# Attention over 1024 positions on one core: two PSUM banks in turn for the projection groups, and the running sum of the probabilities in SBUF

## What is computed

```
B, C, H, W = 16, 512, 32, 32;  N_HEADS = 8;  d_k = 64
xr = x.reshape(B, C, S).transpose(0, 2, 1)                      # S = 1024
q, k, v = split((xr @ w_qkv + b_qkv).reshape(B, S, 8, 192), 3)
attn = softmax(einsum('bihd,bjhd->bijh', q, k) * d_k ** -0.5, over j)
out = einsum('bijh,bjhd->bihd', attn, v).reshape(B, S, 512) @ w_proj + b_proj
return out.transpose(0, 2, 1).reshape(B, C, H, W) + x
```

## Time and profile before

| | |
|---|---|
| median of 2 runs | 3987.8 us (3986.29 to 3989.31) |
| profiled execution | 3987.98 us |
| its span | 3985.9 us |
| granted TensorE clock, mean | 0.997 |

### The profile page before, as it was taken

One profiled execution on the slowest core, in us unless ns is written; L12 is line 12 of the kernel. 1 busy time (PEld: TensorE's weight loads), 2 busy tenths in 40 slices (PEclk: granted clock), 3 DMA queues, 4 the chain that ended last, 5 costly groups with the idle time before them and its releaser, 6 DMA issues.

```text
span 3985.9 us, 60063 instructions
## 1 busy us (share of the span) xinstructions
PE 3936.3 (99%) x18464; PEld 3360.4 (84%) x18464; DVE 3319.5 (83%) x4449; ACT 2935.8 (74%) x5529; POOL 3006.5 (75%) x2371
## 2 busy tenths in 40 slices
PE   8999999999999999999999999999999999999998
PEld 6878888888888888888888888888888888888886
DVE  7788888888888888888888888888888888888887
ACT  5777777777777777777777777777777777777775
POOL 4678777777777777777777777877778777787775
PEclk9999999999999999999999999999999999999999
DMA  6344444434443344443444444444344434444432
GB/s 201 85 108 112 125 107 110 118 95 132 110 120 104 99 131 112 111 113 96 132 105 127 107 107 111 116 128 107 95 121 112 129 100 108 112 110 127 113 93 79
DMA packets 262943, 451.23 MB, mean 113 GB/s; under 512 B 107872, under 2 KB 118112, under 8 KB 258656
## 3 DMA queue, kind: packets, MB, share of 16 engines
q1 hardware_dynamic: 262624, 447.39, 42.4%
HBM read 204.48 MB, written 41.42 MB: 62 GB/s over the span
## 4 chain that ended last, share of the span: by engine, by line
PE 89%; issue 4%; DVE 4%; ACT 2%; DMA 1%; POOL 0%; SPq 0%; ACTq 0%; DVEq 0%
PE ps_g L473 24%; PE s L495 11%; PE ps_o L517 11%; PE ps_o L515 11%; PE st L574 11%; PE st L572 10%; PE ps_g L489 9%; DVE acc L806 2%; PE st L501 1%; PE st L502 1%; ACT p_hl L731 1%; ACT x_h L690 1%; ACT p L728 0%; DVE acc L803 0%; DVE qk_l L787 0%
## 5 line engine op out<-in xcount | busy, mean ns | idle before, releaser
L963 POOL TENSOR_TENSOR p_hl<-p,p_hl 128x512 fp32r<-128x512 f32 x2048 | 2609.0, 1298 | 915.0 <-ACT p_hl L731 914.4
L728 ACT ACTIVATE p<-st 128x512 f32<-128x512 f32 x2048 | 1231.8, 601 | 705.3 <-PE st L574 678.5
L809 DVE TENSOR_REDUCE nm<-s 128x1 fp32r<-128x1024 f32 x1024 | 1250.1, 1221 | 381.6 <-PE s L495 370.8
L806 DVE TENSOR_TENSOR acc<-acc,p 128x512 f32<-128x512 f32 x1792 | 1234.1, 689 | 25.5 <-DVE acc L803 0.5
L731 ACT ACTIVATE p_hl<-st 128x512 fp32r<-128x512 f32 x2048 | 1237.7, 604 | 0.0
L515 PE MATMUL ps_o<-p_hl,v_hl 128*128 128x512 f32 x2048 | 802.9, 392 | 4.5 <-POOL p_hl L963 3.9
L574 PE MATMUL st<-q,k 128*128 128x512 f32 x2048 | 804.4, 393 | 0.0
L517 PE MATMUL ps_o<-p_hl,v_hl 128*128 128x512 f32 x2048 | 802.0, 392 | 0.0
L572 PE MATMUL st<-q,k 128*128 128x512 f32 x2048 | 799.6, 390 | 1.4 <-DVE v_hl L794 1.1
L473 PE MATMUL ps_g<-x_h,wq 128*128 128x512 f32 x2016 | 711.5, 393 | 6.4 <-DVE qk_l L787 6.3
L495 PE MATMUL s<-k,q 128*128 128x512 f32 x2048 | 646.7, 396 | 9.0 <-DMA k<-qk_l 4.7
(11 more groups left out here) (192 smaller groups left out, 3756.8 us busy)
## 6 DMA issues: line engine op xcount, KB each, us to landing
k<-qk_h SPq DMA_DIRECT2D x256, 256.0 KB, 4.3
wq<-wq_d SPq DMA_DIRECT2D x126, 512.0 KB, 4.5
ring<-x_in SPq DMA_DIRECT2D x128, 256.0 KB, 3.7
q<-qk_h SPq DMA_DIRECT2D x128, 256.0 KB, 3.8
q<-qk_l SPq DMA_DIRECT2D x128, 256.0 KB, 4.9
k<-qk_l SPq DMA_DIRECT2D x128, 256.0 KB, 5.1
q<-q SPq DMA_DIRECT2D x256, 128.0 KB, 4.9
rinv<-rinv_d SPq DMA_DIRECT2D x256, 128.0 KB, 2.9
```

The costliest lines, as they stand in the source:

```text
L728: nc.scalar.activation(p[:, to, :], st[slot % RING][:], ACT.Exp)
L806: nc.vector.tensor_tensor(acc[:], acc[:], probs, ALU.add).then_inc(acc_done, 1)
L809: nc.vector.tensor_reduce(nm[:, it:it + 1], s1[:], AXX, ALU.max, negate=True).then_inc(max_done, 1)
L963: nc.gpsimd.tensor_tensor(p_l[:, to, :], p[:, to, :], p_h[:, to, :].bitcast(f32), ALU.subtract).then_inc(pl_done, 1)
```

## The change

`acc` becomes a tile in SBUF, and its bank becomes a second one for groups: `ps_g` is now a list of two. The method `bank` gives the bank of a unit: how many groups begin up to it, modulo 2. `held` becomes a dictionary that keeps, for each bank, the semaphore and the value that its last reader will have set; TensorE waits for it when a group begins in that bank, which is the group before the last one.

```
+        def bank(self, unit):
+
+            return sum(begin <= unit for begin in GROUP) % 2
...
+        acc = sb("acc", [P, HALF])
...
-        acc = ctx.enter_context(nc.psum_tensor("acc", [P, HALF], f32))
-        ps_g = ctx.enter_context(nc.psum_tensor("ps_g", [P, HALF], f32))
-        qk_banks = [ps_o, acc, st[0], st[1]]
-        v_banks = [ps_g, st[2], ps_o, acc]
-        out_banks = [ps_g[:], st[1][:], st[2][:], s1[:, cols(0)], s1[:, cols(1)], ps_o[:], acc[:], st[0][:]]
+        ps_g = [ctx.enter_context(nc.psum_tensor(f"ps_g{i}", [P, HALF], f32)) for i in range(2)]
+        qk_banks = [ps_o, ps_g[1], st[0], st[1]]
+        v_banks = [ps_g[0], st[2], ps_o, ps_g[1]]
+        out_banks = [ps_g[0][:], st[1][:], st[2][:], s1[:, cols(0)], s1[:, cols(1)], ps_o[:], ps_g[1][:], st[0][:]]
...
+            held = {}
+
...
-                held = None if B.first else ("v", 2)
...
-                    if kind and e == 0 and held:
-                        if held[0] == "qk":
-                            pe.wait_ge(l_done, at(16, held[1] + 1))
-                        elif held[0] == "bias":
-                            pe.wait_ge(bias_done, 2)
-                        elif held[0] == "v":
-                            pe.wait_ge(vl_done, at(8, held[1] + 1))
-                        else:
-                            pe.wait_ge(out_ready, at(8, held[1] + 1))
+                    bank = B.bank(U)
+                    if kind and e == 0 and bank in held:
+                        pe.wait_ge(*held[bank])
...
-                        mm = project_qk(ps_g, head, n, part)
+                        mm = project_qk(ps_g[bank], head, n, part)
...
-                        held = (kind, i)
+
+                        held[bank] = {"qk": (l_done, at(16, i + 1)), "v": (vl_done, at(8, i + 1)),
+                                      "out": (out_ready, at(8, i + 1))}[kind]
...
-                        qk_high(head, n, ps_g)
+                        qk_high(head, n, ps_g[B.bank(U)])
...
-                        qk_low(i // 2, i % 2, ps_g)
+                        qk_low(i // 2, i % 2, ps_g[B.bank(U)])
```

More of the change, by code:

```diff
@@ L605, in body @@
                             pe.wait_ge(wv_loaded, at(16 * 2, 16 * (i // 4)))
-                        mm = project_v(ps_g, i % 4, e, lambda i, k: wv[:, i, k, :])
+                        mm = project_v(ps_g[bank], i % 4, e, lambda i, k: wv[:, i, k, :])
                         if e == 1:
@@ L611, in body @@
                             pe.wait_ge(osl_done, at(8, i + 4))
-                        mm = project_out(ps_g, i + 8, part)
+                        mm = project_out(ps_g[bank], i + 8, part)
                         if e == 1:
@@ L615, in body @@
                     if kind:
-                        held = (kind, i)
+                        held[bank] = {"qk": (l_done, at(16, i + 1)), "v": (vl_done, at(8, i + 1)),
+                                      "out": (out_ready, at(8, i + 1))}[kind]
                     if U == BIAS_SUM and B.first:
-                        pe.wait_ge(l_done, held[1] + 1)
+                        if bank in held:
+                            pe.wait_ge(*held[bank])
                         pe.wait_ge(wp_loaded, 16)
@@ L622, in body @@
                             for k in range(KT):
-                                mm = nc.tensor.matmul(ps_g[:, m:m + 1], wp_stage[:, k, m * P:(m + 1) * P], bv[:, k:k + 1],
+                                mm = nc.tensor.matmul(ps_g[bank][:, m:m + 1], wp_stage[:, k, m * P:(m + 1) * P], bv[:, k:k + 1],
                                                       start=k == 0, stop=k == KT - 1)
                         mm.then_inc(bias_summed, 1)
-                        held = ("bias", 0)
+                        held[bank] = (bias_done, 2)
                     if U == 1 and B.first:
@@ L743, in body @@
                             act.wait_ge(pv_done, v)
-                        v_high(i, ps_g)
+                        v_high(i, ps_g[B.bank(U)])
                     if U in WP_SPLIT and B.first:
@@ L900, in body @@
                         dve.wait_ge(bias_summed, 1)
-                        nc.vector.tensor_tensor(bp[:], ps_g[:, 0:KT], bp[:], ALU.add).then_inc(bias_done, 1)
+                        nc.vector.tensor_tensor(bp[:], ps_g[B.bank(BIAS_SUM)][:, 0:KT], bp[:], ALU.add).then_inc(bias_done, 1)
                     kind, i, e = B.group(U)
@@ L904, in body @@
                         dve.wait_ge(h_done, at(16, i + 1))
-                        qk_low(i // 2, i % 2, ps_g)
+                        qk_low(i // 2, i % 2, ps_g[B.bank(U)])
                     if kind == "v" and e == 1:
                         dve.wait_ge(vh_done, at(8, i + 1))
-                        v_low(i, ps_g)
+                        v_low(i, ps_g[B.bank(U)])
                     if kind == "out" and e == 1:
@@ L912, in body @@
                         dve.wait_ge(res_loaded[g % 2], at(16 * KT, 16 * (g // 2 + 1) - 16 * KT))
-                        nc.vector.scalar_tensor_tensor(out=stage[g % 2][:], in0=ps_g[:],
+                        nc.vector.scalar_tensor_tensor(out=stage[g % 2][:], in0=ps_g[B.bank(U)][:],
                                                        scalar=bp[:, g % KT:g % KT + 1], in1=stage[g % 2][:],
```

## The result

The changed kernel takes 4282.62 us (4281.70 to 4283.55, 2 runs) against 3987.8 before, 1.0738 times as long (95% interval 1.0721 to 1.0756): 295 us slower. The forecast was 4300 us, range 4070 to 4620. The number was right. The experiments show that the sum it came from was not: it spread evenly over the program what is lost in some places and not at all in others.

A forecast was written before the change was run, and what follows sets the result against it. TensorE, 99% busy, bounded the kernel before; VectorE was to become the bound. 70 us outside the stretch plus 256 halves of 16.52 us (13.55 work, 2.97 waits) gave 4299, plus 2 us beyond the span: forecast 4300 us, range 4070 to 4620.

The forecast's parts named there:

- Part one: Second PSUM bank for groups: removes TensorE's waits for ps_g, 0 to 28 us, not taken off the forecast time.
- The collision: VectorE operations with two SBUF inputs and GpSimd's share ports as an exclusive lock; whoever comes second is blocked.
- w: Mean wait for GpSimd of each of VectorE's 9 operations per half on acc in SBUF: taken as 0.33 us.
- reading (a): Mean wait if VectorE takes turns with an always busy GpSimd: 2.7 us per half, 0.30 us per operation.
- The copy: VectorE's copy to acc, SBUF to SBUF: left at 685 ns, though the skill's figures suggested 0.27 us less.
- VectorE becomes the bound, and the time is 70 + 256 x (13.55 + 9w): Whole kernel: if the mean wait exceeds 0.19 us, VectorE's work plus nine waits per half sets the time, 4299 us.
- rival 1: GpSimd is the bound: about 45 stretches with split work lose 2.3 or 4.3 us each, about 4140 us; chance 0.13.
- rival 3: VectorE's operations slide into GpSimd's gaps and TensorE's stream stays the bound: 3960 to 3990 us; chance 0.13.
- The path to TensorE: VectorE's lateness reaches TensorE as waits for nm and st_free; waits naming GpSimd's p_hl first would mean rival 1.

The follow-up runs named there:

- e2: Changed kernel, two banks for groups, its 7 additions per half replaced by one-operand reductions of p, sums left out: 3981.3 us, 0.9991.
- e3: Changed kernel, one bank for groups, its 7 additions per half replaced by one-operand reductions of p, sums left out: 3995.5 us, 1.0023.
- e1: Changed kernel with every group in the one bank ps_g[0], acc still in SBUF: 4339.3 us, 1.0886.
- e4: Changed kernel with GpSimd's p_l made for 128 of the 512 columns, additions untouched: 3970.9 us, 0.9961.
- d4: Kernel before, one bank for groups, with the copy and four additions of a half in SBUF (5 of 9 operations can collide): 4152.4 us, 1.0419.
- h1: Changed kernel with VectorE's low part of q and k made for 64 of 512 columns: 4282.7 us, 1.0744.
- i1: Changed kernel with GpSimd's output splits made for 64 of 512 columns: 4177.1 us, 1.0480.
- i2: Changed kernel with GpSimd's input splits made for 64 of 512 columns, VectorE's own kept: 4281.8 us, 1.0741.
- i4: Changed kernel with GpSimd's output splits, input splits and normalisations made for 64 of 512 columns each: 4129.8 us, 1.0361.
- g1: Changed kernel with VectorE's order in a unit turned from addition, maximum, addition to maximum, addition, addition: 4794.5 us, 1.2026.

## Why the prediction was right, and which step failed

**Part one** was priced at 0 to 28 us and is worth 14 where VectorE isn't late (e2 against e3). That its gain doesn't come off the sum was a wrong size: with VectorE late it takes back 57 us (e1), the clock's part included. I had named the second bank's role and put it at zero.

**The collision** is as described: operands decide it (e2: 675 ns with one, 991 with two), the length of GpSimd's operation sets the wait (e4), and VectorE's operation and GpSimd's go in turn. The forecast of 1.0 us for an addition and 1.55 to 1.65 for p_hl met 0.991 and 1.607; w was 0.30 for additions and acc_l, the value of reading (a), where 0.33 was taken.

**The copy** was left at 685 ns. Undisturbed it takes 418 (e4), with its wait 1014: 0.60 us of waiting and 0.27 of gain, together 0.33 more, what was taken for it.

**The step that failed** is "VectorE becomes the bound, and the time is 70 + 256 x (13.55 + 9w)". It put the whole program into one balance. The measured w = 0.30 gives 4230 by it, 53 us short; that 4300 came so close to 4283 is in part the luck of taking 0.33. And d4's own waits give 3979 where 4152 were measured, and 118 us less of VectorE's work change nothing (h1). In the place of one balance there are several. Behind the output splits GpSimd is full, 18.79 of 18.79 us, and with its splits short the loss is gone (i1): that is rival 1, and its 3.5 us at half 4 and 3.9 at 15 and 0 are of the size it named (2.3 to 4.3 a stretch). In four of sixteen halves nothing is lost: that is rival 3's outcome, which I had given 0.13 for the whole, but not its reason. The waits are there (1.12 and 2.38 us in the rows of half 8, some 2.0 us in the half); both engines only have more room there: before the change they were busy for 12.41 and 11.36 us of half 8, against 13.09 and 13.93 of half 4. In 10 and 11 both engines have splits; GpSimd's are worth 0.8 us in 10 and nothing in 11 (i2), and VectorE's two in each half, at 1.77 us apiece, with the addition behind them, make it the fullest engine. In 11 TensorE then waits 1.50 us for the last of them, and in half of the batches its clock falls, which no term of the prediction held. That VectorE's splits are the cause is read from the trace and wasn't tried. The forecast and its rivals were not alternatives but places.

**The path to TensorE** was half right: it waits for nm (75.9 us of PE), as said, but for p_hl about as long (69.7), which the prediction had kept for rival 1; a wait for st_free, also named, is not among its long ones. The chain's share of VectorE is 23%, not a third.

**What stays open:** the 0.5 to 1 us in each of 2, 3, 6, 7 and 14. i4 leaves most of it, so GpSimd's side jobs don't make it. See the last section for what marks these halves and for what the trace of i4 shows in them; no run tried it.

## What to carry to other kernels

Moving an accumulator from PSUM to SBUF frees a bank, and it turns each VectorE operation that then has both operands in SBUF into one that takes turns with GpSimd, and a copy within SBUF as well; count GpSimd's operations beside it before doing so. A wait of this kind is judged stretch by stretch and by what stands in front of it in the queue: a long operation that doesn't collide hides the turn, another colliding one doesn't. A sum over the whole program may give the right time for the wrong reason; a cut of the supposed bound's work (h1) tells in one run whether its busy time is work or waiting.

## What the hardware showed that I hadn't expected

An engine's busy time here contains its blocked time: VectorE went from 83 to 94% and GpSimd from 75 to 88% with no instruction added.

The order of three instructions was worth 512 us with identical work (g1).

A late engine can cost a second time through TensorE's clock: half 11 takes 18.8 us or, with the fall, 20.4, on the same instructions.

The end of a half is slower on VectorE for every second head. In the kernel before, the starts of acc_l, tmp, copy and maximum lie 0.60, 0.61 and 0.59 us apart when tmp's rows are the lower 64 partitions, and 0.72, 0.73 and 0.72 when they are the upper 64:

```profile
432.10 0.69 DVE L814 TENSOR_TENSOR acc_l<-acc,acc_h 128x512 fp32r<-128x512 f32 x1 [0.56 <-ACT acc_h L754]
432.70 0.68 DVE L816 TENSOR_TENSOR tmp<-ps_o,tmp 64x512 f32<-64x512 f32 x1
433.31 0.68 DVE L803 COPY acc<-p 128x512 f32<-128x512 f32 x1
433.90 1.21 DVE L809 TENSOR_REDUCE nm<-s 128x1 fp32r<-128x1024 f32 x1
...
2010.24 0.69 DVE L814 TENSOR_TENSOR acc_l<-acc,acc_h 128x512 fp32r<-128x512 f32 x1 [0.56 <-ACT acc_h L754]
2010.96 0.69 DVE L816 TENSOR_TENSOR tmp<-ps_o,tmp 64x512 f32<-64x512 f32 x1
2011.69 0.70 DVE L803 COPY acc<-p 128x512 f32<-128x512 f32 x1
```

(The maximum behind the last row is in the earlier trace rows, at 2012.41.) The Trainium skill, page "VectorE: DVE Perf Modes", section "Two Vector instructions with no wait between them", says, as a model, that an instruction one of whose inputs or whose output starts in another group of 32 partitions than that of the last instruction to read or write the same memory is held until all earlier ones have finished; the trace agrees with 0.12 us at each of three steps. The halves that end so are 2, 3, 6, 7, 10, 11, 14 and 15, and the small losses that i4 leaves lie in just these.

The trace of i4 shows how 0.12 us can become more. The end of one half of the first kind (tmp's lower partitions), and of one of the second (the upper):

```profile
2105.76 1.02 DVE L816 TENSOR_TENSOR acc_l<-acc,acc_h 128x512 fp32r<-128x512 f32 x1 [0.58 <-ACT acc_h L756]
...
2107.30 0.41 DVE L805 COPY acc<-p 128x512 f32<-128x512 f32 x1
...
2107.53 3.08 POOL L967 TENSOR_TENSOR p_hl<-p,p_hl 128x512 fp32r<-128x512 f32 x2 [1.29 <-ACT p_hl L733]
...
2120.44 1.01 DVE L816 TENSOR_TENSOR acc_l<-acc,acc_h 128x512 fp32r<-128x512 f32 x1 [0.58 <-ACT acc_h L756]
...
2122.21 1.56 DVE L805 COPY acc<-p 128x512 f32<-128x512 f32 x1
...
2122.20 2.72 POOL L967 TENSOR_TENSOR p_hl<-p,p_hl 128x512 fp32r<-128x512 f32 x2 [1.29 <-ACT p_hl L733]
```

GpSimd's next operation begins 1.77 and 1.76 us behind the start of acc_l. The copy begins 1.54 us behind it in the first, ahead of GpSimd, and takes 0.41; in the second it begins at 1.77, the moment GpSimd does, and takes 1.56. Over the 14 batches of i4 the copy takes 0.41 in every half of the first kind and 1.24 to 1.57 on average in 2, 3, 6, 7, 14 and 15 (0.43 in 10 and 11). So a late copy loses its turn. That this makes the whole of the small losses isn't shown: in d4 the copy takes 0.43 in these halves, and they still lose 0.35 to 0.6 us each.
